# Matmuls of zeros in TensorE's planned idle time, in a two-layer attention kernel on one core

## The chip, the core and the metric

The kernel runs on one core of a Trainium2 chip. The metric is the time of one execution on the device, in microseconds (us); lower is better. Five engines work side by side: TensorE (PE in the profile) multiplies matrices into the accumulation banks of PSUM, VectorE (DVE), ScalarE (ACT) and GpSimd (POOL) do the element-wise work, and SyncE (SP) issues most transfers. Each runs its own instructions in order and waits on semaphores that others raise. TensorE's clock is granted by the chip: the profile shows it as a share of full speed, 1.00 (2.4 GHz) or 0.50 (1.2 GHz).

## What is computed

Eight sequences of 1024 tokens by 256 features go through two layers. Each layer adds gated attention over 16 heads of 16 features, and then a gated feed-forward part:

```python
h = _layernorm(x, axis=-1) * (1 + ca) + sa
x = x + ga * _L0_attn_ref(h, L0_attn_W_query, L0_attn_W_key, L0_attn_W_value, L0_attn_W_proj, L0_attn_b_proj)
h = _layernorm(x, axis=-1) * (1 + cb) + sb
x = x + gb * _L0_ffn_ref(h, L0_ffn_W_r, L0_ffn_W_k, L0_ffn_W_v, L0_ffn_mu_r, L0_ffn_mu_k)
```

The second layer has the same frame, with rotary positions in its attention and one linear map (a weight and a low-rank addition to it) as its feed-forward part. Both attentions are causal, with a softmax; the first has a bias that is linear in the distance of two tokens. The outputs are the eight sequences in float32.

## The kernel before

**Units.** One sequence in one layer is a unit, so there are 16 (`UNITS`). After the first and before the last they alternate between layers, which leaves a pattern that repeats every two units, some 352 us.

**Work of TensorE.** In each unit the sixteen heads are taken in four groups. A step `max` (line 1460) computes scores of two heads into two of the three banks of `small`, and VectorE takes their row maxima from there (lines 1267 and 1269) and frees the banks. Those maxima, turned by a transpose (`rows`, line 1469) and split by VectorE into `m_hi` and `m_lo`, go by DMA into the operand `stack_q` (lines 1286, 1287, 910). A step `score` (line 1482) then computes shifted scores into two of the four banks of `big`, ScalarE takes their exponential into `probs` (line 1049), and GpSimd masks the diagonal (line 961). A step `context` (line 1501) multiplies `probs` with the values into `ctx_ps`. Around the attention stand the query and key products (line 1415), the value product (line 1531), the output, gate and feed-forward products (line 1426), and transposes of the normed tokens (line 1515), all into banks of `big`, which ScalarE or VectorE empty. The scores and maxima are float16 products of 64 rows each, two at a time in the two halves of the array; the rest is float32, where the trace has two records for one matmul.

**Layer norm.** VectorE computes the statistics of a unit in one run (lines 1218 to 1248), and ScalarE then writes `xn` (line 1098), which the transposes read.

**What sets the order.** A planner (`plan`, line 343) runs before the program is written. It has a model of the engines (`Model`) with a cost for each step, keeps five queues for TensorE, and takes at each turn the step with the lowest price, a sum of the time that TensorE would wait and of how far the queue lags. `Model.needs` (line 201) says from when a step could run by the model. The list `ITEMS` that comes out is walked once by each engine's program, so every engine's order follows from it. Nothing is decided while the program runs.

**Banks.** `wait_bank` (line 772) makes an engine wait until the next of the four banks of `big` has been emptied. `mask` (line 663) is a bfloat16 tile of 128 by 512, zero in its first 384 columns (lines 937 and 943); VectorE adds it before a maximum.

Of the kernel before, what the change touches and what calls it, by code (L numbers as in the profile page):

```python
# [9 lines left out]
P = 128  # L10
# [5 lines left out]
BANK = 512  # L16
RING = 4
# [153 lines left out]
AHEAD = {"score": 0.0143, "context": 0.0100, "max": 0.8411, "pre": 1.1458, "post": 0.0079}  # L171
EASE, TURN_COST = 500.5758, 138.3034
SEEN, DMA_NS = 251.9964, 495.7496
ROWS_FIRST = 334.5784


class Model:

    def __init__(self):
        self.free = {"PE": 0.0, "ACT": 0.0, "DVE": 0.0, "POOL": 0.0, "SP": 0.0}  # L180
        self.ring, self.small, self.shape = [0.0] * RING, [0.0] * SMALL, None
        self.turn = self.step = 0
        self.ready, self.pipe = {}, 0.0

    def at(self, *keys):
        return max([self.ready.get(k, 0.0) for k in keys], default=0.0)
# [101 lines left out]

    def play(self, item):

        kind, unit = item[0], item[1]
        begin = max(self.free["PE"], self.needs(item))
        shape = self.shape_of(item)
        if shape != self.shape:
            begin, self.shape = begin + TURN_COST, shape
# [47 lines left out]
def plan(model):  # L343
    out, seen, units = [], {("x_load", b) for b in range(STREAMS)}, range(N_UNITS)
# [118 lines left out]
    while any(queues.values()) or later or to_join or to_turn or loads:  # L463
# [4 lines left out]
        for name, queue in queues.items():  # L468
            item = queue[0] if queue else None
            if item and name in ("pre", "post") and (not on_pe(item) or opened not in (None, name) or barred(name, item)):  # L470
                item = None
            if item and name == "score":
                if opened or ("rows", *item[1:3]) not in model.ready or (scored - kept >= HELD and item[6][0] == 0):
                    item = None
            if item and name == "max":
                if ("stack", *item[1:3]) not in model.ready:
                    item = None
                elif left[item[1], item[2]] == 1 and any(k[1] % 2 == item[2] % 2 for k in to_turn):
                    item = None
            if item and name == "context":  # L480
                same = [c for c in contexts[:BURST] if c[1:4] == item[1:4]]
                there = [c for c in same if ("probs", *c[1:5]) in model.ready]
                if not there or there[0] != item or (item[4] == 0 and any(x[2][0] == "save" for x in later)):
                    item = None
                elif len(there) < len(same) and model.shape != 32:
                    item = None
# [22 lines left out]
        name, item = min(options, key=price)  # L509
        if name == "rows":  # L510
            to_turn.pop(0)
        else:
            queues[name].pop(0)
            taken[name] += pe_time(item)
        opened = name if item[0] == "half" else None if name in ("pre", "post") else opened
        model.play(item)
        emit(item, name if name in ("pre", "post") else None)
        if name == "max":
# [109 lines left out]
def adaln_program(nc, x, c0, c1, wmod0, wmod1, wqkv, wout, bias, wffn, mu, lora, wbase, rope, rows_c, out):  # L628
# [14 lines left out]
    with ctx:  # L643
# [19 lines left out]
        mask = sb("mask", [P, BANK], bf16)  # L663
# [51 lines left out]
        big = ctx.enter_context(nc.psum_tensor("big", [P, RING, BANK], f32))  # L715
# [56 lines left out]
        def wait_bank(eng, at, more=0):  # L772

            turn = at.turn() + more
            eng.wait_ge(freed[at.slot(turn)], at.uses(turn) + 1)
# [597 lines left out]
        def _(pe):  # L1373
            te = nc.tensor
# [7 lines left out]
            for c in range(FC):  # L1382
                last = te.matmul(small[:, 2, c * D:(c + 1) * D], lora_2[:, c * P:(c + 1) * P], lora_d,
                                 start=True, stop=True)
# [51 lines left out]
            def step(at, item):  # L1436
                kind, unit = item[0], item[1]
# [3 lines left out]
                if kind == "half":  # L1441

                    item, second = item[2], False
                    kind = item[0]
                    started.add(item)
                elif item in started:
                    first = False
                    started.discard(item)
                if kind == "max":
                    _, _, g, pair, pieces = item  # L1450
                    if (pair, pieces) == (0, MAX_BANKS[0]):

# [159 lines left out]
```

## Time and profile before

| | |
|---|---|
| median of 3 runs | 2933.96 us (2933.64 to 2935.0) |
| the profiled execution | 2937.21 us, its span 2935.4 us |
| TensorE busy (matmuls) | 2480.4 us, 85% of the span |
| VectorE busy | 2340.0 us, 80% |
| ScalarE busy | 1716.9 us, 58% |
| GpSimd busy | 850.4 us, 29% |
| mean granted clock of TensorE | 0.933 |

The span runs from the first to the last instruction. A matmul counts as busy from its start to the modelled end of its way through the array, so matmuls that follow each other overlap in the records, and a busy TensorE isn't at its peak. Busy time is a mean over stages with different limits. The chain of work that ended last is followed back from the last instruction, at each step to what released it.

### The profile page before, as it was taken

The numbers are of one execution on the slowest core, as the hardware profiler recorded it, in microseconds if no ns is written. First come the engines' busy times: TensorE is split into PE (matmuls) and PEld (weight loads), VectorE is DVE, ScalarE is ACT, GpSimd is POOL, SyncE is SP. The second block draws the span as 40 slices with busy tenths as digits, with TensorE's granted clock in tenths as the row PEclk, the third lists the DMA queues.
The fourth block names the chain that finished last, engine by engine and source line by source line (L and its number), as shares of the span: only waits on it lengthen the run. The fifth ranks groups of instructions, "written<-read, shape, count | busy, mean of one in ns | idle before, by whom it ended". The sixth has DMA issues, their size and how long they took to land.

```text
span 2935.4 us, 54933 instructions
## 1 busy us (share of the span) xinstructions
PE 2480.4 (85%) x18968; PEld 1070.4 (36%) x18968; DVE 2340.0 (80%) x7126; ACT 1716.9 (58%) x3458; POOL 850.4 (29%) x954
## 2 busy tenths in 40 slices
PE   5688888988888987988989889798897988988786
PEld 3323433432334333343343334343333433433323
DVE  4598768789887898868988788887888789876793
ACT  2267565556564666556656566665665556656474
POOL 3111341234221342224222252222512234225121
PEclk8789999999999999989999899899998989999898
DMA  5611142113312223212223113231222212301200
GB/s 171 193 38 37 35 123 85 58 46 88 102 41 92 66 66 96 75 61 64 74 88 105 46 48 105 70 93 46 76 88 75 77 64 80 97 28 59 87 14 15
DMA packets 142393, 218.29 MB, mean 74 GB/s; under 512 B 21190, under 2 KB 62556, under 8 KB 142052
## 3 DMA queue, kind: packets, MB, share of 16 engines
q1 hardware_dynamic: 142120, 214.77, 23.7%
q8 instruction: 156, 2.56, 0.4%
q14 instruction: 117, 0.96, 0.1%
HBM read 137.87 MB, written 77.89 MB: 74 GB/s over the span
## 4 chain that ended last, share of the span: by engine, by line
PE 53%; DVE 33%; ACT 6%; issue 4%; DMA 1%; SPq 1%; POOL 0%; DVEq 0%; ACTq 0%; POOLq 0%
PE ctx_ps L1501 12%; DVE small L1269 11%; PE big L1426 10%; PE small L1460 9%; PE big L1482 8%; PE big L1415 7%; DVE mx L1267 5%; PE big L1531 4%; ACT probs L1049 3%; DVE stats L1218 3%; PE big L1515 2%; DVE mx L1269 2%; DVE region L1328 2%; ACT xn L1098 1%; DVE ctx_b L1298 1%
## 5 line engine op out<-in xcount | busy, mean ns | idle before, releaser
L1049 ACT ACTIVATE probs<-big 128x512 f32<-128x512 f32 (+2 forms) x2560 | 1222.9, 565 | 499.6 <-PE big L1482 493.5
L1269 DVE CUSTOM_DVE_ANT_0 small<-small,mask 128x128 f32<-128x128 f32 (+3 forms) x2048 | 941.5, 520 | 107.8 <-PE small L1460 99.6
L1267 DVE TENSOR_REDUCE mx<-small 128x1 f32<-128x512 f32 x1024 | 651.0, 684 | 190.2 <-PE small L1460 183.3
L1482 PE MATMUL big<-stack_q,stack_k 64*128 64x512 f16 (+3 forms) x6144 | 700.0, 332 | 99.7 <-ACT probs L1049 62.8
L961 POOL TENSOR_SCALAR_AFFINE_SELECT probs<-probs 128x512 f32<-128x512 f32 x512 | 331.9, 655 | 1364.4 <-ACT probs L1049 1363.5
L1460 PE MATMUL small<-stack_k,stack_q 64*128 64x512 f16 (+3 forms) x3072 | 473.3, 346 | 237.6 <-DVE mx L1269 154.2
L1501 PE MATMUL ctx_ps<-probs,v_ones 128*17 128x512 f32 (+3 forms) x6144 | 617.9, 499 | 4.1 <-POOL probs L961 3.8
L1460 PEld LDWEIGHTS small<-stack_k,stack_q 64*128 64x128 f16 x3072 | 123.6, 95 | 804.5 <-DVE mx L1269 416.1
L1482 PEld LDWEIGHTS big<-stack_q,stack_k 64*128 64x128 f16 x6144 | 259.5, 95 | 428.9 <-issue 218.0
L1269 DVE DVE_READ_ACCUMULATOR2_ANT mx<- 128x1 f32 x2048 | 285.7, 140 | 0.0
L1415 PE MATMUL big<-hT,w_qkv 128*128 128x512 f32 x512 | 269.0, 637 | 16.4 <-DMA w_qkv<-wqkv 13.4
L1501 PEld LDWEIGHTS ctx_ps<-probs,v_ones 128*17 128x17 f32 x6144 | 121.5, 96 | 277.2 <-issue 165.4
L1098 ACT ACTIVATE xn<-x_res,nmr,rstd 128x256 f32<-128x256 f32 x256 | 129.2, 587 | 149.2 <-DVE nmr L1239 149.2
L1021 POOL TENSOR_TENSOR region<-region 128x512 f16<-128x512 f32 x128 | 145.7, 1157 | 227.6 <-ACT region L1091 227.6
L1075 ACT ACTIVATE region<-big 128x512 f32<-128x512 f32 x128 | 75.6, 595 | 197.8 <-PE big L1415 197.8
L1531 PE MATMUL big<-w_qkv,hT 128*128 128x128 f32 x1024 | 146.0, 290 | 1.9 <-ACT probs L1049 0.6
L1298 DVE STREAM_TRANSPOSE ctx_b<-ctx_u 128x512 f32<-128x512 f32 x128 | 90.3, 706 | 70.1 <-ACT ctx_u L1059 67.5
L1426 PE MATMUL big<-w_out,ctxT 128*128 128x256 f32 x512 | 128.1, 413 | 16.4 <-DVE ctxT L1309 10.7
L1426 PE MATMUL big<-w_ffn,region 128*128 128x256 f32 x512 | 127.2, 408 | 15.7 <-DVE region L1328 15.2
L1531 PEld LDWEIGHTS big<-w_qkv,hT 128*128 128x128 f32 x1024 | 126.0, 196 | 27.3 <-issue 15.7
L1059 ACT ACTIVATE ctx_u<-ctx_ps 128x512 f32<-128x512 f32 x128 | 78.8, 615 | 80.8 <-PE ctx_ps L1501 80.3
L1415 PEld LDWEIGHTS big<-hT,w_qkv 128*128 128x128 f32 x512 | 85.2, 192 | 102.2 <-issue 87.4
(91 smaller groups left out, 1958.6 us busy)
## 6 DMA issues: line engine op xcount, KB each, us to landing
image<-region SPq DMA_DIRECT2D x192, 256.0 KB
stack_q<-image SPq DMA_DIRECT2D x64, 512.0 KB, 3.6
stack_k<-image SPq DMA_DIRECT2D x64, 512.0 KB, 4.6
lo_dram<-region SPq DMA_DIRECT2D x64, 256.0 KB
w_qkv<-wqkv SPq DMA_DIRECT2D x16, 768.0 KB, 4.8
x_res<-x SPq DMA_DIRECT2D x32, 256.0 KB, 5.0
stack_q<-lo_dram SPq DMA_DIRECT2D x128, 64.0 KB, 3.9
stack_k<-lo_dram SPq DMA_DIRECT2D x128, 64.0 KB, 4.6
```

The lines of the kernel that those rows point to most:

```text
L961: g.affine_select(out=diag, in_=diag, compare_op=ALU.is_ge, fill=0.0, base=0, pattern=[[0, GH], [1, P]], channel_multiplier=-1).then_inc(m ...
L1021: g.tensor_tensor(lo, own, hi, ALU.subtract).then_inc(split_done, 1)
L1049: s.activation(probs[:, n % HELD, heads, q0:], big[:, at.slot(turn), 0:len(pairs) * width] .rearrange("p (h q) -> p h q", h=len(pairs)), A ...
L1098: ins = s.activation(xn[:, t, :], x_res[:, batch % STREAMS, t, :], ACT.Identity, scale=rstd[:, t:t + 1], bias=nmr[:, t:t + 1])
L1267: last = v.reduce_max(to, held, AX)
L1269: last = v.tensor_tensor_reduce(out=held, in0=held, in1=mask[:, BANK - width:], scale=1.0, scalar=3.0 * NEG, op0=ALU.add, op1=ALU.max, acc ...
L1415: last = te.matmul(big[:, at.slot(), :], w[:, c, ft * P:(ft + 1) * P], rhs[:, c, tb * BANK:(tb + 1) * BANK], start=(c == 0), stop=(c == FC ...
L1426: last = te.matmul(big[:, at.slot(), t * D:(t + 1) * D], lhs[:, c, (n * 2 + t) * P:(n * 2 + t + 1) * P], w[:, c, :], start=(c == 0), stop= ...
L1460: last = te.matmul(small[:, at.small(parity), col:col + width], stack_q[rows, 0, g * PAIR_N + pair, qt * P:(qt + 1) * P], stack_k[rows, 0, ...
L1482: last = te.matmul(big[:, at.slot(at.turn() + parity), j * width:(j + 1) * width], stack_k[rows, c, g * PAIR_N + pair, kt * P:(kt + 1) * P ...
L1501: last = te.matmul(ctx_ps[32 * h:32 * h + DH + 1, q0:], v_ones[:, (2 * unit + g // 2) % V_HALVES, kt, (g % 2) * GH + h, :], probs[:, n % H ...
L1531: last = te.matmul(big[:, at.slot(), j * P:(j + 1) * P], h_all[:, c, t * P:(t + 1) * P], w_qkv[:, 2, c, half * P:(half + 1) * P], start=(c ...
```

## The change

While it plans, the model now keeps a list of the times in which TensorE worked (`worked`). Before each step that TensorE takes, `Model.warm` compares the time from which the step can run with the time at which TensorE comes free. If the wait is 500 ns or more, the next bank of `big` is free by the model, and TensorE's modelled busy share over the last `WINDOW` nanoseconds is 0.6 or less, an entry `warm` goes into the list ahead of the step. It holds a number of matmuls, the wait less 150 ns divided by 165 ns. TensorE's program carries them out: it waits for the next bank of `big`, and multiplies zeros of `mask` (384 columns, bfloat16) into that bank as often as the entry says. The bank isn't taken; the next step that uses it overwrites it. The rows and columns of the array follow the step before: 64 rows after a score or a maximum, 32 columns after a context step, else all. No other engine does anything for such an entry.

```diff
--- before.py
+++ after.py
@@ -171,6 +171,8 @@
+WARM_WAIT, WARM_BUSY = 500.0000, 0.6000
+WARM_NS, WINDOW = 165.0, 3413.0
@@ -181,6 +183,13 @@
+        self.worked = []
+
+    def busy(self, now):
+
+        while self.worked and self.worked[0][1] < now - WINDOW:
+            self.worked.pop(0)
+        return sum(min(b, now) - max(a, now - WINDOW) for a, b in self.worked if a < now) / WINDOW
...
@@ -288,8 +297,23 @@
     def play(self, item):
 
+        self.take(item)
+        self.worked.append((self.began, self.free["PE"]))
+
+    def warm(self, until):
+
+        wait = until - self.free["PE"]
+        if wait < WARM_WAIT or self.ring[self.turn % RING] > self.free["PE"] or self.busy(until) > WARM_BUSY:
+            return 0
+        n = int((wait - 150) / WARM_NS)
+        self.worked.append((self.free["PE"], self.free["PE"] + n * WARM_NS))
+        self.free["PE"] += n * WARM_NS
+        return n
+
+    def take(self, item):
...
@@ -513,6 +537,9 @@
+        idle = model.warm(model.needs(item))
+        if idle:
+            out.append(("warm", item[1], idle, model.shape or 128))
         model.play(item)
...
@@ -1446,7 +1473,14 @@
-                if kind == "max":
+                if kind == "warm":
+
+                    wait_bank(pe, at)
+                    rows, cols = slice(0, 64 if item[3] == 64 else P), slice(0, 32 if item[3] == 32 else P)
+                    for _ in range(item[2]):
+                        te.matmul(big[cols, at.slot(), 0:BANK - P], mask[rows, cols], mask[rows, 0:BANK - P],
+                                  start=True, stop=True)
+                elif kind == "max":
```

The steps that the planner puts in the list, and their order, are the same as before but for the new entries. There are 62 of them, with 687 matmuls in all. Their sizes: 24, 10, 22, 52 and 18 matmuls in the first two units before any maximum is taken; then nineteen of 4 to 6 between the steps `max` of the first unit and ahead of its first `score`; 36 in each of five units, behind the last scores before a layer norm of the repeating pattern; 15, 48, 28, 16 and 19 around the last unit; and 28 others of 2 to 16.

The first place is in the program's beginning, on TensorE, where the query and key products of the second unit (`hT`, `w_qkv`) end and the first maxima (`small`) begin. Before:

```order
L1515 MATMUL big<-ident,xn 128x128 x16
L1415 MATMUL big<-hT,w_qkv 128x512 x8
L1460 MATMUL small<-stack_k,stack_q 128x128 x2
L1460 MATMUL small<-stack_k,stack_q 128x384 x2
L1415 MATMUL big<-hT,w_qkv 128x512
```

and now:

```order
L1549 MATMUL big<-ident,xn 128x128 x16
L1481 MATMUL big<-mask 128x384 x52
L1442 MATMUL big<-hT,w_qkv 128x512 x8
L1481 MATMUL big<-mask 128x384 x18
L1494 MATMUL small<-stack_k,stack_q 128x128 x2
L1494 MATMUL small<-stack_k,stack_q 128x384 x2
L1442 MATMUL big<-hT,w_qkv 128x512
```

52 matmuls of zeros stand ahead of the eight products, and 18 between these and the first step `max`.

The second place is on TensorE in the fifth unit, where it stands still while VectorE computes a layer norm; `ident,mxc` is the transpose of the maxima, `probs,v_ones` a context step. Before:

```order
L1469 MATMUL big<-ident,mxc 32x128
L1501 MATMUL ctx_ps<-probs,v_ones 17x512 x8
L1482 MATMUL big<-stack_q,stack_k 128x512 x4
L1460 MATMUL small<-stack_k,stack_q 128x256 x4
L1482 MATMUL big<-stack_q,stack_k 128x512 x8
L1460 MATMUL small<-stack_k,stack_q 128x512 x4
```

and now:

```order
L1503 MATMUL big<-ident,mxc 32x128
L1535 MATMUL ctx_ps<-probs,v_ones 17x512 x8
L1516 MATMUL big<-stack_q,stack_k 128x512 x4
L1481 MATMUL big<-mask 128x384 x36
L1494 MATMUL small<-stack_k,stack_q 128x256 x4
L1516 MATMUL big<-stack_q,stack_k 128x512 x8
L1494 MATMUL small<-stack_k,stack_q 128x512 x4
```

36 matmuls of zeros stand between the last `score` step and the `max` step behind it; the same rows stand at four later places.

The third place is the end of TensorE's program, with the last unit's output product (`w_out,ctxT`), its transposes and its feed-forward product (`w_ffn,hT`). Before:

```order
L1501 MATMUL ctx_ps<-probs,v_ones 17x128 x4
L1426 MATMUL big<-w_out,ctxT 128x256 x16
L1515 MATMUL big<-ident,xn 128x128 x16
L1426 MATMUL big<-w_ffn,hT 128x256 x16
L643 UNCONDITIONAL_BRANCH
```

and now:

```order
L1535 MATMUL ctx_ps<-probs,v_ones 17x128 x4
L1481 MATMUL big<-mask 32x384 x16
L1453 MATMUL big<-w_out,ctxT 128x256 x16
L1549 MATMUL big<-ident,xn 128x128 x16
L1481 MATMUL big<-mask 128x384 x19
L1453 MATMUL big<-w_ffn,hT 128x256 x16
L670 UNCONDITIONAL_BRANCH
```

16 matmuls of zeros (32 columns of the array) stand ahead of the output product, and 19 between the transposes and the last product.

## Rows read from the trace of the kernel before

**Rows 1.** The page: TensorE's granted clock in 40 slices, and the chain by engine.

```profile
PEclk8789999999999999989999899899998989999898
PE 53%; DVE 33%; ACT 6%; issue 4%; DMA 1%; SPq 1%; POOL 0%; DVEq 0%; ACTq 0%; POOLq 0%
```

**Rows 2.** Busy time by stretch (columns: PE, PEld, DVE, ACT, POOL, clock, DMA), first unit.

```profile
117.70:121.00 3.30, 3.30 (x14) 2.06 (x13) 2.23 (x10) 0.50 (x1) 0.00 (x0) 0.50 0.66 189
...
131.30:157.60 26.30, 13.07 (x58) 4.59 (x58) 24.03 (x72) 0.60 (x1) 0.00 (x0) 0.50 0.23 73
157.70:165.30 7.60, 6.90 (x43) 2.22 (x39) 6.47 (x27) 4.58 (x10) 1.27 (x2) 0.50 0.01 2
```

**Rows 3.** The same view, around a layer norm in the fifth unit's attention.

```profile
916.40:919.70 3.30, 1.06 (x13) 0.41 (x6) 3.30 (x6) 1.63 (x4) 0.00 (x0) 1.00 0.00 0
919.80:923.10 3.30, 3.30 (x10) 2.58 (x9) 2.04 (x5) 0.19 (x1) 0.00 (x0) 0.50 0.00 0
947.10:950.40 3.30, 1.06 (x12) 0.11 (x4) 3.23 (x17) 1.08 (x2) 0.00 (x0) 1.00 0.78 258
950.50:953.80 3.30, 0.00 (x0) 0.00 (x0) 2.82 (x18) 0.29 (x1) 0.00 (x0) 0.50 0.90 303
953.90:964.10 10.20, 8.23 (x40) 3.02 (x40) 7.41 (x30) 8.01 (x16) 0.63 (x1) 0.50 0.04 9
```

**Rows 4.** Timeline (start, us, engine, line, op, [idle before]) of ACT and TensorE there.

```profile
919.40 6.92 PE L1426 MATMUL big<-w_ffn,region 128*128 128x256 f32 x23 [2.24 <-DVE region L1328]
...
945.66 1.08 ACT L1049 ACTIVATE probs<-big 128x512 f32<-128x512 f32 x2 [7.63 <-PE big L1482]
...
954.32 0.61 PE L1460 MATMUL small<-stack_k,stack_q 64*128 64x256 f16 x4 [6.16 <-DVE mx L1269]
```

**Rows 5.** Chain that ended last: the pieces after 919.40, then shares of 953.9 to 964.1.

```profile
919.40 8.86 PE big L1426 x32
...
by line: PE big L1482 24.8%; PE big L1515 18.6%; DVE small L1269 17.7%; PE ctx_ps L1501 17.6%; PE small L1460 15.6%; DVE m_lo L1287 2.8%; DVE mx L1269 2.4%; issue 2.3%; DVE m_hi L1286 1.4%
```

**Rows 6.** Timeline of TensorE: steps of the maxima, and scores back to back, at two clocks.

```profile
154.25 0.61 PE L1460 MATMUL small<-stack_k,stack_q 64*128 64x512 f16 x2 [0.82 <-DVE mx L1267]
155.68 0.61 PE L1460 MATMUL small<-stack_k,stack_q 64*128 64x512 f16 x2 [0.82 <-DVE mx L1267]
...
835.17 0.39 PE L1460 MATMUL small<-stack_k,stack_q 64*128 64x512 f16 x2 [0.81 <-DVE mx L1267]
836.38 0.39 PE L1460 MATMUL small<-stack_k,stack_q 64*128 64x512 f16 x2 [0.82 <-DVE mx L1267]
...
955.62 1.89 PE L1482 MATMUL big<-stack_q,stack_k 64*128 64x512 f16 x8 [0.69 <-DVE m_lo L1287]
...
2785.14 1.03 PE L1482 MATMUL big<-stack_q,stack_k 64*128 64x512 f16 x8
```

**Rows 7.** Timeline of TensorE where zeros go in and the trace has no idle time.

```profile
102.39 0.39 PE L1460 MATMUL small<-stack_k,stack_q 64*128 64x128 f16 x4
...
157.64 1.94 PE L1482 MATMUL big<-stack_q,stack_k 64*128 64x512 f16 x8
```

**Rows 8.** Timeline of TensorE at the end of the program.

```profile
2920.22 3.48 PE L1515 MATMUL big<-ident,xn 128*128 128x128 f32 x16 [11.85 <-ACT xn L1098]
2924.84 7.15 PE L1426 MATMUL big<-w_ffn,hT 128*128 128x256 f32 x32 [1.14 <-ACT hT L1066]
```

**Rows 9.** Busy time by stretch, three other stretches that follow a block.

```profile
670.60:677.30 6.70, 6.16 (x16) 1.46 (x20) 6.15 (x16) 2.95 (x7) 5.24 (x4) 0.50 0.00 0
...
2760.50:2776.50 16.00, 12.48 (x48) 6.44 (x48) 12.02 (x37) 6.29 (x11) 4.95 (x4) 0.50 0.00 0
...
2899.50:2902.80 3.30, 3.19 (x8) 2.59 (x9) 0.01 (x1) 0.00 (x0) 0.00 (x0) 0.50 0.00 0
```

**Rows 10.** Busy time by stretch: transposes alone on TensorE, and just after them.

```profile
76.70:80.00 3.30, 3.30 (x16) 3.09 (x15) 0.00 (x0) 2.12 (x3) 0.00 (x0) 0.50 0.58 192
80.10:83.40 3.30, 0.09 (x1) 0.00 (x0) 0.00 (x0) 0.89 (x2) 0.00 (x0) 1.00 0.65 223
```

More of the change, by code:

```diff
@@ L289, in play @@
     def play(self, item):
+        self.take(item)
[9 more added lines that the diff above has]
+    def take(self, item):
         kind, unit = item[0], item[1]
         begin = max(self.free["PE"], self.needs(item))
+        self.began = begin
         shape = self.shape_of(item)
```

## The prediction

> **What bounds the kernel now.** I read the chain that ended last first: TensorE holds 53% of it and VectorE 33%, and transfers 1% [rows 1]. So TensorE's rate counts for half of the time, and nearly all the rest is VectorE's. Then the granted clock by slice: it is below full speed in about a third of the slices [rows 1], 0.933 in the mean. With only two levels, 1.00 and 0.50, that is 0.067 x 2 = 13% of the time at half speed, some 395 us. Then busy time in short stretches, where the clock is seen to fall after TensorE has stood still or nearly so: it is 1.00 while TensorE works 1.06 of 3.3 us, 0.50 in the next 3.3 us without work, and stays at 0.50 for the 10.2 us of real work behind them [rows 3]. The change can only gain there: what real work ran at 0.50 behind an idle time, on the path.
>
> **What one matmul of zeros costs.** The trace has none. The nearest rows are float16 scores in the same 64 rows of the array. Four pairs of 512 columns take 1.03 us at full clock, one pair alone 0.39, so a pair follows the last after (1.03 - 0.39) / 3 = 0.213 us; at half clock (1.89 - 0.61) / 3 = 0.427 us [rows 6]. With 384 columns it is three quarters: 0.16 us at full clock, 0.32 at half. The first pair's record ends some 0.17 us after the array could take the next (0.39 - 0.213), so the room for zeros is the idle time plus 0.17 us. No other engine reads or waits for the zeros. The added wait for a bank should cost nothing: at the block of 36, the bank's last reader on ScalarE ends at 945.66 + 1.08 = 946.74 us, before TensorE falls idle at 948.2 (954.32 - 6.16) [rows 4].
>
> **Blocks that fit.** 36 matmuls take 5.8 us at full clock, and the idle time is 6.16 us, ended by VectorE's maxima behind the layer norm [rows 4]. The same gap stands five times, within 0.01 us. Between the maxima, 5 zeros take 0.80 us in 0.82 + 0.17 [rows 6]. At full clock these cost nothing. If the cover goes, each costs its overrun, and the next step on TensorE and the VectorE that waits for it are late by as much.
>
> **Blocks that don't fit.** The 18 ahead of the first `max` step find no idle time: the step starts at 102.39 us right behind the product before it [rows 7]. VectorE has nothing to do until that step is done, so 18 x 0.16 = 2.9 us go to the path in full (ends 0 and 5.8, at half clock). The 4 ahead of the first `score` (157.64 us) find none either [rows 7], 0.65 us; a few others are too long by 0.2 to 0.6 us; I take 1.7 us for all of these, ends 0 and 3.5. The last block matters most: 19 zeros take 3.0 us, the idle time ahead of the last product is 1.14 us, and that product ends the program [rows 8]. That is 3.0 - 1.3 = 1.7 us at full clock and up to 3.5 where the clock comes back later behind the transposes than it did here; I take 2.5. Sum of the costs: 7.1 us.
>
> **What the clock gives back,** place by place, with VectorE's idle share as a cap where it is the next bound.
> - First unit. 117.7 to 121.0 us is all TensorE at 0.50 [rows 2]: 3.3 / 2 = 1.65 us. From 131.3 to 157.6 us VectorE looks full (24.03 of 26.3 us), but a step of two maxima repeats after 1.43 us at half clock (155.68 - 154.25) and after 1.21 us at full (836.38 - 835.17) [rows 2, 6]. Some 16 steps x 0.22, and one value product of 2 us at half clock, give 4.5 us. From 157.7 to 165.3 TensorE works 6.90 of 7.6 us and VectorE 6.47 [rows 2]: between 1.1 and 3.4, I take 2.5. Together 8.7 us.
> - The five blocks of 36. Behind them 10.2 us run at 0.50; TensorE has 77% of the chain there (24.8 + 18.6 + 17.6 + 15.6), so halving it would give 3.9 us, but VectorE is busy 7.41 us [rows 3, 5], which caps the gain at 2.8. I take 2.5 each, 12.5 us, ends 1.0 (the clock falls again one stretch later) and 2.8.
> - Five blocks of 3 near 917 us. Behind them the feed-forward products, pure TensorE on the path, ran 3.3 us at 0.50 [rows 3, 5]: 1.7 us each if the clock holds. Three zeros add 0.48 us to 1.06 us of work in the stretch that decides, with 2.24 us idle [rows 3, 4]; the trace doesn't show what suffices, so I count half, 4.3 us, ends 0 and 8.5.
> - 670.6 to 677.3 us: TensorE 6.16 of 6.7, VectorE 6.15 [rows 9]; I take 2 (0.5 to 3).
> - The end. 2760.5 to 2776.5 us, VectorE 12.02 of 16 [rows 9]: a cap of 4, which I take. 2899.5 to 2902.8, output product alone: 1.6 us.
>
> These make 33.1 us. A fifth goes off, 6.6 us, since the chain is one path and part of each gain is handed to VectorE or ScalarE work that lay close behind it, and since the clock now falls in other places than before (its falls are tied to the chip's time, not to the program). 33.1 - 6.6 - 7.1 = 19.4 us. The profiled execution took 2937.2 us (span 2935.4), 3.2 us over the median of the runs; it becomes 2917.8 us, and the median 2933.96 - 19.4 = 2914.6 us. With all ends together the gain is 1 to 38 us.
>
> **A rule against it.** Sixteen transposes alone on TensorE, 3.30 of 3.3 us at 0.50, are followed by 1.00 [rows 10]; so matmuls count for the clock even where they only move data. The Trainium skill (TensorE: Matmul & The Clock Gate, Part 4, PE-mode transpose) says that in transpose mode the full clock does not engage, as it doesn't count as busy in the same way. By that rule the clock would have stayed low at 80.1 us; the trace disagrees. What it would mean for zeros, that matmuls without real products don't hold the clock, is the second rival below, 2973 us.
>
> **Rivals.**
> 1. *The gains are absorbed.* VectorE is busy 80% of the span and has a third of the chain [rows 1]. If it or ScalarE takes over everywhere, a third of 33 us is left, 11, less 7 of cost: 2930 us. The step of 1.21 against 1.43 us speaks against it [rows 6].
> 2. *Zeros don't hold the clock* (slower). Then it falls 2.3 us into each block of 36, at 950.5 as before [rows 3]: 14 at 0.16 and 22 at 0.32 make 9.3 us in 6.3 of room, 3.0 us late, five times, 15 us. Seventeen blocks between maxima of the first unit take 1.6 us in 1.0, 10 us. The 48 in the last unit are late by 3, the ones that don't fit cost 10 rather than 7, and other small blocks 1: 39 us, 2973 us. It decides where the clock between 950.5 and 953.9 is 0.50. For it: nothing in the trace shows zeros, and one block fills half of the array's rows, where pairs filled both. Against it: [rows 10].
> 3. *Blocks meet a low clock by position* (slower). The gains shift every later step against the clock's own rhythm; a block that starts at half clock overruns by its length. If one block of 36 does (36 x 0.32 = 11.5 us in 6.3 of room, 5 us) and a third of the some 36 short ones (0.6 us each, 7 us), and half of the 33 us is lost: 16.5 - 7.1 - 12 = -2.6, 2937 us. It decides where such blocks start at 0.50. Against it: ahead of the blocks of 36 TensorE works at 1.00 [rows 3].
> 4. *It doesn't do what it says*: the trace's idle times aren't where the model has them. That holds for 18 zeros and the few above, and is in the sum.
>
> **How the numbers follow.** Forecast 0.70 (2896 to 2928 us), rival 1 0.13 (2928 to 2935), rival 3 0.09, rival 2 0.08. About 0.2%, 5.9 us, is what a measurement of this kernel can tell from no change. Faster by more: 0.70 and a little of rival 1, 0.72; slower by more: rival 2 and part of rival 3, 0.12; the rest, 0.16, within. The range is 2896 to 2937 us: it leaves out rival 2, half of rival 3 and the gains above 38 us.
>
> **What the new profile would show.** A mean clock near 0.96 (0.933 now). At each block of 36: TensorE busy 5.8 us, clock 1.00 behind it, and the next `max` step no later behind its VectorE maximum than before. Steps of 1.21 us in the first unit from 131 us on. The first `max` step 2.9 us later than the product before it. An idle time ahead of the last product that has gone, and that product 2 to 3 us later behind the transposes. The prediction is wrong if the clock falls within blocks, if the idle time of VectorE grows by as much as TensorE's steps shrink, or if the 10.2 us stretches shorten by less than 1 us.

## The result, and the profile after

The changed kernel takes 2915.65 us, the median of 9 runs (2907.4 to 2923.5), against 2933.96 us for the kernel before on the same chip (9 runs, 2924.6 to 2939.5). The ratio is 0.9939, with a 95% interval of 0.9924 to 0.9954: 17.9 us, or 0.6%, faster. Its profiled execution took 2919.2 us, with a span of 2917.5 us, 17.9 us below the span before. The mean granted clock went from 0.933 to 0.957.

The page of the changed kernel: granted clock by slice, the chain by engine, and the group of the zero matmuls (count | busy us, mean ns | idle before).

```profile
PEclk9999999999989999999999999999998999999999
PE 53%; DVE 33%; ACT 7%; issue 4%; DMA 1%; SPq 1%; POOL 1%; DVEq 0%; ACTq 0%; POOLq 0%
L1481 PE MATMUL big<-mask 64*128 64x384 bf16 (+2 forms) x687 | 130.6, 340 | 1.5 <-DVE hT L1204 1.5
```

Two slices of 40 are left below 0.9 of full speed, where [rows 1] had ten. The chain has nearly the same shares as before (ScalarE and GpSimd one point more each): the change made the path faster without moving it to another engine. VectorE is busy for as long as before (2338.9 us, 2340.0 before), so its idle time fell with the span. Zeros hold the clock. The timeline of TensorE shows a block of 36 (start, us, engine, line, op, idle before), and the windows show the stretches in it and behind it (PE, PEld, DVE, ACT, POOL busy, clock, DMA):

```profile
945.97 6.01 PE L1481 MATMUL big<-mask 64*128 64x384 bf16 x36
952.30 0.39 PE L1494 MATMUL small<-stack_k,stack_q 64*128 64x256 f16 x4 [0.32 <-DVE mx L1296]
```

```profile
948.50:951.80 3.30, 3.30 (x22) 1.79 (x19) 2.82 (x18) 0.31 (x1) 0.00 (x0) 1.00 0.94 322
951.90:962.10 10.20, 8.05 (x79) 3.05 (x81) 9.78 (x35) 9.50 (x20) 1.63 (x3) 1.00 0.08 26
```

The block fits: 0.32 us of idle time is left behind it, and the next `max` step isn't late. The 10.2 us behind it are now at 1.00 ([rows 3] had 0.50), and VectorE, busy for 7.41 of 10.2 us there before, is now busy for 9.78. It is the next bound, which is why the gain was capped. At the third and the fifth of these places the gain was smaller, since the clock fell for 3.4 us a little behind the block. At the third, the block of 36 starts at 1645.3 us:

```profile
1655.20:1658.60 3.40, 3.40 (x22) 2.06 (x24) 2.25 (x7) 3.00 (x6) 0.64 (x1) 0.50 0.04 7
```

Steps of the maxima in the first unit now follow each other after 1.20 us instead of 1.43 [rows 6], with five zeros in each gap:

```profile
140.21 0.97 PE L1481 MATMUL big<-mask 64*128 64x384 bf16 x5
141.19 0.39 PE L1494 MATMUL small<-stack_k,stack_q 64*128 64x512 f16 x2
141.41 0.97 PE L1481 MATMUL big<-mask 64*128 64x384 bf16 x5
142.39 0.39 PE L1494 MATMUL small<-stack_k,stack_q 64*128 64x512 f16 x2
```

The two places without room are late, as [rows 7, 8] said: 18 zeros ahead of the first `max` step, and 19 ahead of the last product, which now starts 7.07 us after the transposes do (2907.03 - 2899.96) instead of 4.62 [rows 8].

```profile
103.01 3.09 PE L1481 MATMUL big<-mask 128*128 128x384 bf16 x18
106.03 0.39 PE L1494 MATMUL small<-stack_k,stack_q 64*128 64x128 f16 x4
...
2899.96 3.68 PE L1549 MATMUL big<-ident,xn 128*128 128x128 f32 x16 [11.85 <-ACT xn L1125]
2903.43 3.77 PE L1481 MATMUL big<-mask 128*128 128x384 bf16 x19
2907.03 7.07 PE L1453 MATMUL big<-w_ffn,hT 128*128 128x256 f32 x32
```

One gain isn't there. Three zeros stand ahead of the feed-forward products near 917 us, and the product still takes 8.86 us, as in [rows 5]; the clock falls as it begins:

```profile
914.96 0.65 PE L1481 MATMUL big<-mask 64*128 64x384 bf16 x3
917.36 8.86 PE L1453 MATMUL big<-w_ffn,region 128*128 128x256 f32 x32 [1.76 <-DVE region L1355]
```

```profile
914.40:917.70 3.30, 1.54 (x17) 0.71 (x10) 3.30 (x6) 1.59 (x3) 0.00 (x0) 1.00 0.02 5
917.80:921.10 3.30, 3.30 (x10) 2.65 (x9) 2.01 (x5) 0.42 (x1) 0.00 (x0) 0.52 0.00 0
```

**The whole difference, place by place.** The same step can be found in both timelines, and the difference of its starts tells how far the changed kernel is ahead (negative) or behind. The feed-forward product, for example, starts at 917.36 here and at 919.40 before: -2.0. Read along the program, with the times of the kernel before:

| stretch (us) | difference at its ends | change | predicted |
|---|---|---|---|
| start, to 101 (with the blocks of 24, 10, 22 and 52) | 0 to +0.7 | +0.7 | 0 |
| 18 zeros, 102 | +0.7 to +3.6 | +2.9 | +2.9 |
| first unit, 115 to 175 | +3.6 to -3.4 | -7.0 | -8.7 +1.7 (part of the 1.7 is for blocks further on) |
| 175 to 600 | -3.4 to -2.1 | +1.3 | |
| 600 to 680 | -2.1 to -4.0 | -1.9 | -2.0 |
| 680 to 840 | -4.0 to -2.0 | +2.0 | |
| five blocks of 36 | 3.2, 3.0, 1.8, 3.2, 1.9 | -13.1 | -12.5 |
| five blocks of 3 at 917 and so on | none | 0 | -4.3 |
| the rest, 840 to 2752 | | +3.0 | |
| 2752 to 2785 | -12.1 to -16.9 | -4.8 | -4.0 |
| 2785 to 2905 | -16.9 to -20.3 | -3.4 | -1.6 |
| 19 zeros, the end | -20.3 to -17.8 | +2.5 | +2.5 |

The lines without a forecast are what the prediction had taken off as a fifth, 6.6 us; together they are 6.3. But this is one execution, and other traces show how much of it is chance. The kernels e3, e5 and e6 below are the changed kernel up to 805 us, with the same zeros. Between 103 and 800 us their leads grow by 13.1, 13.2 and 13.5 us, where this trace gains 8.3 (+3.6 to -4.7). The start scatters as well: at 101 us the traces of this document lie between 1.2 us ahead of the kernel before and 6.0 behind it.

### The profile page after: what moved, and what is told of

It is laid out like the page before. It is cut to its first block, busy times and chain, and to the rows that moved or that the text cites. A ratio compares the mean times of both kernels' runs of the same rounds, so it can differ in the third digit from the quotient of the medians.

```text
span 2917.5 us, 56308 instructions
## 1 busy us (share of the span) xinstructions
PE 2560.3 (88%) x19655; PEld 1120.4 (38%) x19655; DVE 2338.9 (80%) x7126; ACT 1715.2 (59%) x3458; POOL 851.9 (29%) x954
## 4 chain that ended last, share of the span: by engine, by line
PE 53%; DVE 33%; ACT 7%; issue 4%; DMA 1%; SPq 1%; POOL 1%; DVEq 0%; ACTq 0%; POOLq 0%
PE ctx_ps L1535 13%; DVE small L1296 11%; PE big L1453 10%; PE big L1516 8%; PE small L1494 8%; PE big L1442 7%; DVE mx L1294 4%; PE big L1565 4%; ACT probs L1076 3%; DVE stats L1245 2%; PE big L1549 2%; DVE mx L1296 2%; DVE region L1355 2%; ACT xn L1125 2%; DVE ctx_b L1325 1%
## 5 line engine op out<-in xcount | busy, mean ns | idle before, releaser
L1494 PE MATMUL small<-stack_k,stack_q 64*128 64x512 f16 (+3 forms) x3072 | 466.4, 339 | 170.0 <-DVE mx L1296 96.0
L1453 PE MATMUL big<-w_ffn,region 128*128 128x256 f32 x512 | 129.1, 413 | 13.2 <-DVE region L1355 12.7
L1481 PE MATMUL big<-mask 64*128 64x384 bf16 (+2 forms) x687 | 130.6, 340 | 1.5 <-DVE hT L1204 1.5
L1453 PE MATMUL big<-w_out,ctxT 128*128 128x256 f32 x512 | 120.7, 396 | 11.4 <-DVE ctxT L1336 10.7
```

The source lines that it names most:

```text
L1453: last = te.matmul(big[:, at.slot(), t * D:(t + 1) * D], lhs[:, c, (n * 2 + t) * P:(n * 2 + t + 1) * P], w[:, c, :], start=(c == 0), stop= ...
L1494: last = te.matmul(small[:, at.small(parity), col:col + width], stack_q[rows, 0, g * PAIR_N + pair, qt * P:(qt + 1) * P], stack_k[rows, 0, ...
```

## The experiments

All kernels below compute the whole result; only blocks of zeros are left out, added or resized, or their matmuls given other rows. The blocks are numbered in the order of the program, from 0 to 61, and resized in the list that the planner made, so no other step moves. Each kernel has 4 to 11 runs, beside runs of the kernel before, whose medians on those chips were 2932.3 to 2936.6 us; I compare by ratios, and turn a difference of ratios into us with 2936 us (0.001 is 2.9 us). Single runs of one kernel spread over 4 to 16 us, so a difference of 3 us between two kernels decides nothing, and the trace has to.

### One part undone or alone

**e1: the blocks that don't fit are left out** (the 18, the 4 ahead of the first `score`, one of 2, one of 8, and the last 19).

```diff
+def resize(items, size):
+    out, n = [], 0
+    for item in items:
+        if item[0] == "warm":
+            if size(n, item):
+                out.append(("warm", item[1], size(n, item), item[3]))
+            n += 1
+        else:
+            out.append(item)
+    return out
+
+ITEMS = resize(ITEMS, lambda n, item: 0 if n in (4, 23, 30, 32, 61) else item[2])
```

> The changed kernel without the five blocks that found no or too little idle time: the 18 zeros ahead of the first maxima, the 4 ahead of the first scores, the 2 and the 8 in the middle, and the 19 ahead of the last product. Theory (a block without room costs its own length on the path): in the trace of the changed kernel the first maxima are 2.9 us later behind the 18, and the last product 2.4 us later behind the 19; with some 1 us for the others the kernel should take 6 us less than the changed one, 2909 to 2910 us against 2915.7, and about 0.8% less than the kernel before. Rival (the idle time only moves, since VectorE sets the pace in the first unit): 2.4 us at the end alone, 2913 us.

2906.87 us, ratio 0.9906 (0.9892 to 0.9921): 9.7 us better than the change. In its trace the first `max` step is no longer late (the difference stays at 1.0 us across it), and neither is the last product (+0.1 across it, where the change has +2.5). These are the 5.4 us that the two long misfits cost. The remainder comes from places without a misfit, for instance 4.4 us between 300 and 600 us (this trace gains 3.3 there, the changed kernel's loses 1.1). e3, e5 and e6 have every block of the changed kernel in that stretch and gain 1.5, 1.7 and 2.5 us there: in the traces it is the changed kernel's execution that fell badly, and not the misfits. By the runs the remainder is 4.3 us, no more than their spread. e4 shows how such a difference can come about.

**e2: only the five blocks of 36.**

```diff
+ITEMS = resize(ITEMS, lambda n, item: item[2] if item[2] == 36 else 0)
```

> Only the five blocks of 36 are kept, all other zeros are gone. Theory (each holds the clock over a layer norm, and the 10 us of real work behind it run at full clock): the changed kernel's trace gains 3.2, 3.0, 1.8, 3.2 and 1.9 us behind these blocks, so 13 us less than the kernel before, 2921 us. Rival (part of what the trace shows there is chance, since the low stretches come elsewhere instead): 5 to 8 us less, 2926 to 2929 us.

2921.93 us, ratio 0.9949 (0.9937 to 0.9961), 15 us less than before; in the trace the blocks bring 3.2, 3.1, 3.0, 3.2 and 3.1 us, 15.6 in all. They are worth what the cap by VectorE says (2.8), or a little more. It also tells what the changed kernel's third and fifth block missed (1.8 and 1.9).

**e4: only the first 24 blocks, those of the first unit.**

```diff
+ITEMS = resize(ITEMS, lambda n, item: item[2] if n < 24 else 0)
```

> Only the 24 blocks up to the first scores are kept (281 matmuls of zeros... the first five blocks and the nineteen of 4 to 6), the rest of the program is as before. Theory (the first unit gains 7 us by 175 us into the program, as in the changed kernel's trace, and these stay): 2927 us. Rival (the gain is lost again where later falls of the clock come at other places, as the changed kernel's trace shows 1.6 us lost at 280 to 316 us): 2929 to 2931 us.

2933.38 us, ratio 0.9990 (0.9981 to 0.9999), some 3 us less than before. The trace is 4.2 us ahead at 175 us and 3.0 at the end. What lies between is the same program without a single zero, yet its lead grows to 6.0 us at 820 and is 4.0 at 840. There, in this kernel (first line) the clock is lower over the same 54 matmul records than in the kernel before (second line):

```profile
823.80:836.00 12.20, 9.15 (x54) 2.74 (x58) 9.40 (x27) 8.24 (x18) 2.43 (x3) 0.58 0.12 32
```

```profile
829.80:840.00 10.20, 7.11 (x54) 2.38 (x58) 9.05 (x27) 8.14 (x18) 2.42 (x3) 0.83 0.05 6
```

The same work, 6 us earlier, gets 0.58 instead of 0.83 and takes 2.0 us longer. So a fall of the clock is not a property of the place in the program alone. The reading that fits is that it also counts where the idle time lies in the chip's time, so that any gain upstream reshuffles the later falls. (The expectation's 281 matmuls of zeros are 224; its argument doesn't use the number.) At this place the changed kernel loses 2.4 us (-4.4 to -2.0); 2.0 of that come without any block there. Of the changed kernel's blocks of 5 near 830 us, which meet the low clock and overrun, only some 0.4 us is left to explain. That is a comparison of single traces: e6, without these blocks, loses nothing there, and neither does e3, which has them.

**e6: seven small late blocks left out** (8, and six of 5).

```diff
+ITEMS = resize(ITEMS, lambda n, item: 0 if n in (32, 33, 34, 37, 40, 43, 46) else item[2])
```

> The changed kernel without the blocks of 5 between maxima at 831, 1196, 1548, 1899 and 2251 us and the 8 at 807 us. In the changed kernel's trace 2.2 to 2.5 us of the gain are lost at three of these places, where the clock stays at half for 10.2 us and not for 3.4. Theory A (the zeros run at half clock there and overrun their 0.8 us, 0.6 to 0.8 us each time, and the rest is the clock's): 2 to 3 us less than the changed kernel, 2913 us. Theory B (all of the loss is where the fall lies in the clock's rhythm): no difference, 2916 us. Theory C (the zeros help the clock up more than they cost): 2 us more, 2918 us.

2910.16 us, ratio 0.9917 (0.9901 to 0.9933), 6.5 us better than the change where 2 to 3 were expected of costs. The excess can't be booked to the blocks: 5.2 us of this trace's advantage over the changed kernel's arose between 103 and 800 us, ahead of the first block that was left out.

### One size changed

**e5: 18 zeros instead of 36.**

```diff
+ITEMS = resize(ITEMS, lambda n, item: 18 if item[2] == 36 else item[2])
```

> The changed kernel with 18 zeros in place of 36 at the five long blocks, so that they end some 3.3 us before the next step instead of 0.3. Theory A (what counts is that the idle time is filled to its end: the clock falls in the idle rest and the work behind runs at half clock): the 13 us of the blocks are mostly lost, 2926 us. Theory B (half a block is enough to bring the clock over the idle time): no difference to the changed kernel, 2916 to 2918 us. Where the fall comes depends on where the idle rest lies in the chip's own rhythm, so the five places may differ among themselves; then it comes out between.

2925.80 us, ratio 0.9962 (0.9949 to 0.9976), 6.8 us worse than the change. That is less than the 13.1 us that the five blocks had brought, because this trace was further ahead before it reached them (7.7 us ahead of the kernel before at 840 us, the changed kernel's 2.0, with the same zeros). At the blocks themselves, half a block brings nothing: the lead is 7.6 us ahead of the first block and 7.4 behind it, 7.3 and 7.2 at the second. After 3.24 us without work the next step starts at half clock, and the 10.2 us behind it stay there:

```profile
940.35 3.09 PE L1495 MATMUL big<-mask 64*128 64x384 bf16 x18
946.68 0.60 PE L1508 MATMUL small<-stack_k,stack_q 64*128 64x256 f16 x4 [3.24 <-DVE mx L1310]
```

```profile
946.70:956.90 10.20, 8.64 (x42) 3.14 (x44) 6.97 (x28) 7.57 (x15) 0.64 (x1) 0.50 0.02 4
```

**e3: 13 zeros instead of 3 ahead of the feed-forward products.**

```diff
+ITEMS = resize(ITEMS, lambda n, item: 13 if n in (35, 38, 41, 44, 47) else item[2])
```

> The changed kernel with 13 zeros in place of 3 at the five places ahead of the gate products, where TensorE stands idle for 2.2 us and the clock fell in the changed kernel as in the one before. Theory (3 zeros were too few, 13 fill the idle time and hold the clock; the products behind are TensorE's alone and on the path): 3.4 us at half clock become 1.7, five times, 8.5 us less than the changed kernel, 2907 us. Rival (the clock falls there for what lies ahead of the gap, or the work behind waits for VectorE anyway): no difference, 2915 us.

2909.59 us, ratio 0.9917 (0.9903 to 0.9931), 6.5 us better. The product takes 7.17 us instead of 8.86, five times, which is the 1.7 us each that the prediction gave for a clock that holds:

```profile
908.21 2.27 PE L1495 MATMUL big<-mask 64*128 64x384 bf16 x13
```

```profile
910.62 7.17 PE L1467 MATMUL big<-w_ffn,region 128*128 128x256 f32 x32
```

That is 8.5 us. But each block of 36 now gained only 0.7 to 0.9 us, 4.0 together instead of 13.1, since the clock was at 0.50 for 6.8 us behind each of them:

```profile
938.20:944.60 6.40, 5.74 (x37) 3.02 (x35) 5.82 (x36) 2.17 (x6) 0.00 (x0) 1.00 0.85 281
944.90:951.70 6.80, 5.69 (x28) 2.73 (x28) 4.60 (x18) 5.68 (x11) 0.64 (x1) 0.50 0.01 2
```

The two nearly cancel in this trace. What it is ahead of the changed kernel's it had before its first difference: 8.8 us against 2.0 at 840 us. So the price of the products is shown on the spot, and the total doesn't confirm it.

**e7: longer and more blocks, and no misfits:** the long idle times are filled in full.

```diff
+    more = {2853: 46, 3760: 46, 4667: 46, 5574: 46, 2928: 15, 3835: 15, 4742: 15, 5649: 15}
+    size = {0: 50, 3: 80, 4: 0, 23: 0, 30: 0, 31: 55, 32: 0, 59: 25, 61: 0, 35: 13, 38: 13, 41: 13, 44: 13, 47: 13}
...
+        if i == 7274:
+            out.append(("warm", item[1], 72, 128))
```

> A version that may beat both: without the five blocks that found no room, 13 zeros at the gate products, 25 in place of 28, and zeros also where the trace shows long idle times that the planner didn't fill: 50 and 80 in place of 24 and 52 in the first two units, 55 in place of 6 ahead of the layer norm at 796 us, 46 at the four like it (1154, 1502, 1855 and 2202 us), 15 behind each, 72 in the idle time ahead of the last transposes. Theory (gains add up as long as the clock was low behind each idle time): 9 us from the blocks without room, 6 from the gate products, five times 2.5 behind the second kind of layer norm, four times 1 behind the 15, 2 to 3 at either end of the program: some 34 us less than the changed kernel, 2882 us, with a mean clock of 0.985. Rival (VectorE takes over, gains beyond the changed kernel's halve): 17 us less, 2899 us.

2896.08 us, ratio 0.9858 (0.9843 to 0.9874), 41.7 us less than before by the ratio, and nearer to the rival's 2899 than to the theory's 2882. What is missing is plain in the trace: behind each block of 36 the clock still falls for 6.8 us, though TensorE stands still for only 0.32 us there, and for 0.91 us one step later, as in the changed kernel. That left two suspects: where the blocks lie in the chip's time, and what the zeros are made of.

### The rows of the array

**e8: the changed kernel, with every matmul of zeros in all 128 rows** instead of the 64 of the scores. **e9: the same of e7.**

```diff
-                    rows, cols = slice(0, 64 if item[3] == 64 else P), slice(0, 32 if item[3] == 32 else P)
+                    rows, cols = slice(0, P), slice(0, 32 if item[3] == 32 else P)
```

> The changed kernel, but every matmul of zeros fills all 128 rows of the array and not the 64 of one half (same count, same columns, same time). In the traces so far the clock rose within 24 zeros of 128 rows, but not within 8 of 64 rows, and it fell behind some blocks of 36 with 64 rows when little real work followed. Theory A (half of the array counts for less): the clock holds at more places, among them behind the 5 zeros between maxima at 831, 1548 and 2251 us, the mean clock goes from 0.957 to 0.965 or more, and the kernel takes 4 to 8 us less, 2908 to 2912 us. Theory B (rows don't matter): clock and time as in the changed kernel, 2916 to 2918 us.

> The version with more and longer blocks (e7_more), again with all 128 rows in every matmul of zeros. In e7_more the clock still fell behind each block of 36 (6.8 us at half clock), so those blocks gained 0.8 us each and not 3. Theory A (half of the array counts for less): these falls go, 5 x 2 us and the like elsewhere, 2880 to 2886 us, mean clock 0.985. Theory B (rows don't matter): as e7_more, 2896 us.

e8: 2899.29 us, ratio 0.9875 (0.9857 to 0.9893), 18.8 us better than the change. e9: 2882.10 us, ratio 0.9816 (0.9802 to 0.9831), 12.3 us better than e7, and 53.7 us less than the kernel before by the medians. No other version is faster beyond the spread of the runs. A block takes as long as before (36 in 6.02 us), and the number of zeros is the same. What differs is the clock behind the block, in e7 (first pair) and e9 (second pair):

```profile
931.50:938.00 6.50, 6.18 (x42) 3.40 (x39) 5.92 (x36) 2.06 (x4) 0.00 (x0) 1.00 0.87 295
938.90:945.70 6.80, 5.71 (x28) 2.74 (x28) 4.61 (x18) 5.65 (x11) 0.64 (x1) 0.51 0.01 2
```

```profile
931.80:938.20 6.40, 6.40 (x40) 3.46 (x40) 5.82 (x33) 1.61 (x4) 0.00 (x0) 1.00 0.93 303
938.30:948.50 10.20, 8.19 (x78) 3.15 (x82) 9.78 (x35) 9.37 (x20) 1.85 (x3) 1.00 0.02 5
```

At each of the five places the lead grows by 0.8 us in e7 and by 3.1 in e9 (means): 2.3 us more, or some 11.7 us of the 12.3 (the two profiled executions are 16.6 us apart in all).

Is it the rows, or where the blocks lie in the chip's time? All traces together can tell. With 64 rows, eight kernels (the changed one, e1, e2, e3, e6, e7, e10, e11) have 40 places with a block of 36: the clock fell for 6.8 us behind it at 14 of them (all five of e3 and of e7, one of e10, three of e11), for 3.4 us at 2, and not at all at 24. With all rows, e8, e9 and e12 have 15 such places: never for 6.8 us, once for 3.4 (the fourth of e12). And in three traces the first block lies alike behind the clock's last rise: it starts 112.0 us behind it in e3 (825.5 to 937.5 us), in e7 (819.5 to 931.5) and in e12 (826.2 to 938.15). The clock fell behind it in e3 and e7, with 64 rows, and held in e12, with all. So zeros in half of the rows count for less towards the clock. They do count: 36 of them held it at most places. All rows don't help everywhere: in e8 three zeros held the clock ahead of the first feed-forward product (7.17 us), and not ahead of the other four:

```profile
907.32 7.17 PE L1453 MATMUL big<-w_ffn,region 128*128 128x256 f32 x32 [1.65 <-DVE region L1355]
```

```profile
1245.89 8.86 PE L1453 MATMUL big<-w_ffn,region 128*128 128x256 f32 x32 [1.65 <-DVE region L1355]
```

Three are too few at nine of ten places (five of the changed kernel, four of e8), and thirteen were enough even in 64 rows (e3 and e7, ten of ten).

**e12: e9 without the six small blocks of e6 that it still has.**

```diff
-    size = {0: 50, 3: 80, 4: 0, 23: 0, 30: 0, 31: 55, 32: 0, 59: 25, 61: 0, 35: 13, 38: 13, 41: 13, 44: 13, 47: 13}
+    size = {0: 50, 3: 80, 4: 0, 23: 0, 30: 0, 31: 55, 32: 0, 33: 0, 34: 0, 37: 0, 40: 0, 43: 0, 46: 0, 59: 25, 61: 0,
+            35: 13, 38: 13, 41: 13, 44: 13, 47: 13}
```

> This is e9 (all the longer blocks, every matmul of zeros in all 128 rows) without the block of 5 near 819 us and the five blocks of 5 that stand between the maxima near 821, 1176, 1520, 1866 and 2210 us. Theory A (small late blocks only cost): leaving them out of the kernel after gained 6.4 us (e6), but half of that came from one block of 8 that e9 doesn't have any more; with them gone from e9, 0 to 3 us come back and the time is 2880 us (2878 to 2883). Theory B (in all 128 rows the small blocks help to hold the clock): in e9 the clock is high at four of the five places (a fall only at 814.8); without them it falls there as in the kernel before, 1.5 to 2.5 us at each, and the time is 2890 us (2886 to 2894).

2880.98 us, ratio 0.9826 (0.9811 to 0.9842), 2.9 us worse than e9 by the ratio and 1.1 better by the medians: no difference that these runs can tell. Theory B's 2890 is out. Once the long idle times are filled, what the small blocks cost or bring is within some 3 us.

### Is a cost on the path always a cost?

e1 had gained more than its blocks cost, and in several traces the repeat of two units took either some 348.5 or some 351.7 us (the kernel before has 351.8, 351.7, 351.2, 351.9). That was read too neatly, as the changed kernel has 348.7, 350.6, 348.9 and 350.8. It suggested that falls pull the program onto the chip's time, so that small delays are swallowed. The test is a known delay on top of e1: zeros at four places where TensorE has work on both sides and nothing waits.

```diff
+def late(items, count):
...
+        if item[0] == "half" and item[2][0] == "key" and item[2][2:] == (0, 0) and item[1] in (5, 7, 9, 11):
+            out.append(("warm", item[1], count, 128))
```

> e1_fit_only with 6 more zeros, 0.96 us at full clock, between the gate and the key products of four repeats, where TensorE alone sets the pace and has no idle time. In the traces the pattern of two units takes 351.6 us in some kernels and 348.2 in others, with nothing between, whatever the zeros save. Theory A (the falls of the clock come with the chip's rhythm and pull the pattern onto it): the delay is swallowed, the repeat stays at 348.2 us, and the time is that of e1_fit_only within 1 us, 2908 us. Theory B (costs add up): 4 x 0.96 = 3.8 us more, 2912 us. Theory C (the pattern is tipped over to the next value, 351.6 us): 14 us more, 2921 us.

> As e10_late_6 with 12 zeros, 1.92 us, at each of the four places. Theory A (swallowed): 2908 us. Theory B (costs add up): 4 x 1.92 = 7.7 us more than e1_fit_only, 2915 us. Theory C (tipped over to 351.6 us a repeat): 14 us more, 2921 us.

e10 (6 zeros each): 2912.01 us, ratio 0.9918 (0.9905 to 0.9932), 3.5 us above e1; e11 (12 each): 2916.08 us, ratio 0.9939 (0.9924 to 0.9953), 9.7 above e1. Bare addition gives 3.8 and 7.7. The total of e10 lies within the spread of the runs, and that of e11 rules out a delay that is swallowed (0), but hardly one that tips the repeat over (14). The traces decide: at each of the four places the lead shrinks by 0.97 us in e10 and by 1.95 in e11, in full. e11 lost more elsewhere, some 2 us at each of the three blocks of 36 behind which its clock fell. My theory of the swallowed delay fell: on the path, a delay counts in full.

## Why the prediction was right

**The time.** Forecast 2914.6 us, measured 2915.65. The mechanism was right: zeros in idle time cost nothing, held the clock, and were paid for where no idle time lay under them. The steps were not all as good as the sum: 4.3 us too much at the blocks of 3 were made up in part by 2.6 too little at the end and 0.6 at the blocks of 36, and that the sum came within 1.1 us is luck. (The prediction's third of the slices below full speed is ten of 40 below 0.9 [rows 1]; nothing was worked out from it.)

**What one zero costs** was right: 0.16 us at full clock (36 in 6.01 with the last one's way through the array), 0.32 at half, and nothing where it lies in idle time (e2's five blocks leave the next step on time). Reading it from back-to-back scores [rows 6] was enough.

**Blocks that don't fit:** 2.9 and 2.5 us, as forecast, and e1 takes both away. The working, overrun = zeros less idle time where the next step ends the path, can be used as it is.

**The blocks of 36:** 13.1 us against 12.5, and the cap was the right reading: VectorE's 7.41 busy us of 10.2 [rows 3] left 2.8 to gain, and it is now nearly full. Where the clock held throughout, the gain was 3.0 to 3.2, a little over the cap; where it fell again for 3.4 us, 1.8 and 1.9. So the 2.5 was a mean of two kinds of places. e2 and e5 confirm the mechanism from both sides.

**First unit:** 7.0 us net, against 8.7 less 1.7; e3, e4, e5 and e6, with the same zeros there, have 7.0 or 7.1. **670, 2760 and 2899 us:** 1.9, 4.8 and 3.4 against 2, 4 and 1.6; the last was too small, as the fall at 2841 to 2872 us that disappears as well wasn't counted (1.6 to 1.8 us).

**The step that failed** is "five blocks of 3 near 917 us", counted at half of 8.5. The prediction said that the trace doesn't show what suffices, and took the middle. The clock fell at all five: 0. e3 shows that 8.5 was the right price on the spot and that more zeros would have bought it. Where five like places repeat, all or nothing, 8.5 or 0, was likelier than a half, and either would have said more than the middle.

**The fifth taken off** met its size (6.3 us against 6.6) by luck: some 5 us of the 6.3 arose ahead of 800 us in this one execution, and e3, e5 and e6, with the same zeros there, don't have them. No run shows the term by itself. Of its two reasons e4 supports one, falls that come at other times over work that has no zeros in it. The other reason, gains handed to VectorE, was already in the caps, and no run shows it separately.

**Rivals.** The first (gains absorbed, 2930) is out: the time lies 14 us below it, the chain's shares hardly changed, and VectorE's idle time fell. The second (zeros don't hold the clock) is out as worded, since 1.00 stands between 948.5 and 951.8 us; but the caveat beside it, that one block fills only half of the rows, was worth some 12 us, as e9 against e7 shows, and should have been a case of its own. The sixteen transposes of [rows 10], behind which the clock rose, pointed the right way: matmuls that only move data, and zeros, count for the clock. The third (blocks meet a low clock) happened only on a small scale: the blocks of 36 all started at 1.00.

**What stays open.** e1 and e6 each gained some 4 us more than their blocks cost, which I put down to where the falls came in those runs; traces of the same zeros differ by 5 us by 800 us, and the runs' own spread is as large. That the chip's time is the cause of it is argued and not shown: no experiment moved a kernel in it by a known amount to test it. Why the clock held behind the 64-row blocks of 36 at 24 places and fell for 6.8 us at 14 is open too, except that these are shifted in time.

## What to carry to other kernels

Where TensorE works on the path behind an idle time and its clock is at half, the price of the idle time is read from the stretch behind it: half of TensorE's share, capped by the idle share of the next engine. Matmuls of zeros into a free bank buy it back, if they fill the whole idle time (36 did, 18 did nothing), best in all 128 rows, and end before the next step is released; a block with no idle time under it costs its full length. Since a gain can move later falls, judge such a change by several runs and by the trace's lead at each place, not by one total.

## What the runs showed of the hardware

**Rows count for the clock.** The same 36 matmuls of zeros in the same 6.0 us are followed by a fall of 6.8 us at 14 of 40 places in 64 rows, and at none of 15 in 128. The times agree: 12.3 us less (e9 against e7), and 18.8 us less (e8 against the change), though e8 may owe a part to the next point.

**VectorE's smallest operations wait for GpSimd.** In the kernel before, a layer norm ends with operations on 8 columns. While GpSimd runs its products over 512 columns, most of these take as long as GpSimd's own operations. VectorE first, then GpSimd:

```profile
1157.10 0.17 DVE L1242 TENSOR_TENSOR tmp<-rstd 128x8 f32<-128x8 f32 x1
...
1159.74 1.19 DVE L1242 TENSOR_TENSOR tmp<-rstd 128x8 f32<-128x8 f32 x1
1160.96 1.18 DVE L1244 TENSOR_TENSOR tmp<-tmp,ve 128x8 f32<-128x8 f32 x1
1162.18 1.19 DVE L1246 TENSOR_SCALAR tmp<-tmp 128x8 f32<-128x8 f32 x1
```

```profile
1157.74 1.26 POOL L966 TENSOR_TENSOR w_out<-w_out,gates 128x512 f32<-128x512 f32 x1
...
1160.87 4.91 POOL L981 TENSOR_TENSOR x_res<-x_res,bias_bc 128x512 f32<-128x512 f32 x4
```

TensorE stands still for 7.67 us at that place. In e8 GpSimd came late once, held by a transfer, when the layer norm was nearly done:

```profile
1139.79 0.17 DVE L1269 TENSOR_TENSOR tmp<-rstd 128x8 f32<-128x8 f32 x1
1139.99 0.17 DVE L1271 TENSOR_TENSOR tmp<-tmp,ve 128x8 f32<-128x8 f32 x1
1140.19 0.17 DVE L1273 TENSOR_SCALAR tmp<-tmp 128x8 f32<-128x8 f32 x1
```

```profile
1140.39 1.30 POOL L993 TENSOR_TENSOR w_out<-w_out,gates 128x512 f32<-128x512 f32 x1 [1.07 <-DMA bias_bc<-bias]
```

TensorE then waited 2.03 us instead of 7.67, and the lead grew by 5.7 us across that one place. So part of what e8 gained in its profile was this, not the clock. The Trainium skill (Advanced Engine Details and Errata, VectorE Performance Modes, Mode Summary) says that GpSimd's instructions and some of VectorE's block each other, as they share a port. The trace agrees that they hold each other up, and gives it a size of 1.2 us for an operation of 0.17; that the port is the reason no run here shows. It stands four times in the repeating pattern: running GpSimd's seven products after the layer norm may gain up to 5.7 us each, an estimate from this one place, and has nothing to do with the clock. I didn't try it.
